# A three-step gate on the output projection of a four-batch attention and MoE block

## The reference, cut to what matters

```python
h = _layernorm(x) * (1 + ca) + sa
x = x + ga * attention(h)            # out @ out_w + out_b at its end
h = _layernorm(x) * (1 + cb) + sb
x = x + gb * ffn(h)                  # top-4 routing, 16 experts, shared expert
```

## Time and profile before

| what | value |
|---|---|
| median of three runs | 3380.76 us |
| the profiled execution | 3378.87 us |
| its span, first to last instruction | 3377.1 us |
| PE busy | 88% of the span |
| DVE, ACT, POOL busy | 66%, 53%, 39% |
| mean granted TensorE clock | 0.939 |
| mean DMA rate | 106 GB/s |

### The profile page before, as it was taken

The page is one execution under the profiler, slowest core; times in us unless marked ns, Lnnn a source line. Parts: engine busy times, 40 slices in busy tenths (PEclk is TensorE's granted clock), DMA queues, the critical chain, the costliest instruction groups (busy, mean ns, idle before and its releaser), DMA issues.

```text
span 3377.1 us, 61010 instructions
## 1 busy us (share of the span) xinstructions
PE 2970.4 (88%) x22500; PEld 1632.5 (48%) x22500; DVE 2242.5 (66%) x5047; ACT 1782.1 (53%) x2736; POOL 1311.7 (39%) x1685
## 2 busy tenths in 40 slices
PE   7787799999999999999988878888877799999886
PEld 4433233334333333333333222227876788999775
DVE  7887498888788877999877756413821124655465
ACT  3322456665666655666544545664644465666322
POOL 6755112134322145211357446334045514441355
PEclk9988899999999999999989878998989899999998
DMA  4833512232222223122324332134355545564465
GB/s 162 209 99 101 116 33 57 62 79 63 68 60 63 60 57 92 43 38 61 76 87 127 93 97 84 51 126 143 91 161 166 163 124 167 179 182 143 143 178 150
DMA packets 290690, 359.05 MB, mean 106 GB/s; under 512 B 65404, under 2 KB 243212, under 8 KB 290140
## 3 DMA queue, kind: packets, MB, share of 16 engines
q1 hardware_dynamic: 259516, 279.94, 30.3%
q0 software_dynamic: 30208, 71.87, 7.0%
q10 hardware_dynamic: 672, 3.34, 0.4%
HBM read 206.25 MB, written 139.21 MB: 102 GB/s over the span
## 4 chain that ended last, share of the span: by engine, by line
PE 52%; DVE 12%; ACT 9%; issue 7%; POOL 3%; DMA 3%; SPq 3%; another core or an unknown queue 2%; POOLq 0%; ACTq 0%; DVEq 0%
PE PB L1139 12%; PE PB L1066 8%; PE PB L1155 8%; ACT P L1615 8%; DVE mx L1434 7%; PE PB L1013 6%; PE PB L1036 5%; PE PB L1049 5%; PE PB L1124 2%; PE PB L1080 2%; DMA ON<-osb 1%; SPq L844 1%; PE PB L1103 1%; POOL P L1762 1%
## 5 line engine op out<-in xcount | busy, mean ns | idle before, releaser
L1434 DVE TENSOR_REDUCE mx<-PB 128x1 f32<-128x512 f32 (+3 forms) x2560 | 1405.8, 603 | 293.1 <-PE PB L1013 155.5
L1615 ACT ACTIVATE P<-PB 128x1024 f32<-128x1024 f32 (+3 forms) x1280 | 1097.8, 894 | 791.9 <-PE PB L1049 771.7
L1013 PE MATMUL PB<-KO,QO 64*128 64x512 bf16 (+3 forms) x2560 | 782.2, 359 | 81.6 <-DVE mx L1434 56.5
L1066 PE MATMUL PB<-P,V 128*17 128x512 f32 (+3 forms) x5120 | 617.7, 555 | 15.6 <-POOL P L1762 15.6
L1036 PE MATMUL PB<-QO,KO 64*128 64x512 bf16 (+3 forms) x2560 | 550.7, 359 | 54.4 <-ACT P L1615 28.9
L1049 PE MATMUL PB<-QO,KO 34*128 34x512 bf16 (+3 forms) x2560 | 543.0, 359 | 42.7 <-remote 29.5
L1013 PEld LDWEIGHTS PB<-KO,QO 64*128 64x128 bf16 x2560 | 205.5, 94 | 769.7 <-DVE mx L1434 545.0
L1545 DVE TENSOR_TENSOR haT<-sl,PB 64x128 f32<-64x128 f32 x350 | 101.4, 290 | 556.7 <-ACT sl L1694 357.7
L1139 PE MATMUL PB<-xT,ws 128*128 128x128 f32 x3432 | 451.3, 284 | 19.3 <-issue 10.7
L1139 PEld LDWEIGHTS PB<-xT,ws 128*128 128x128 f32 x3432 | 425.1, 200 | 23.8 <-issue 13.0
L1762 POOL TENSOR_SCALAR_AFFINE_SELECT P<-P 128x256 f32<-128x256 f32 x512 | 205.3, 410 | 572.6 <-ACT P L1615 568.4
(11 more groups left out here) (179 smaller groups left out, 3328.5 us busy)
## 6 DMA issues: line engine op xcount, KB each, us to landing
xq<-x_slots SPq DMA_DIRECT2D x286, 128.0 KB
qk_parts<-pt SPq DMA_DIRECT2D x192, 128.0 KB, 2.4
KO<-qk_parts SPq DMA_DIRECT2D x192, 128.0 KB, 3.8
y_slots<-yo SPq DMA_DIRECT2D x191, 128.0 KB
QO<-qk_parts SPq DMA_DIRECT2D x64, 256.0 KB, 3.6
rden<-rden_rows SPq DMA_DIRECT2D x256, 64.0 KB
y_slots<-mx SPq DMA_DIRECT2D x95, 128.0 KB
v_rows<-vst SPq DMA_DIRECT2D x16, 544.0 KB, 3.5
```

Source lines behind the costliest of these rows:

```text
L1013: mm = pe.matmul(PB[:, bank, 0:n], QO[half, k3, j, 128 * t:128 * t + 128], KO[half, k3, j, 512 * kc:512 * kc + n], start=True, stop=True)
L1066: mm = pe.matmul(PB[32 * j:32 * j + 17, 7, c0:512], V[:, g % 2, kt, 17 * j:17 * j + 17], P[:, pbuf(g, i, j // 2), j % 2, 0:n], start=kt == ...
L1434: dve.tensor_reduce(mx[:, j, t, kc:kc + 1], PB[:, u.bank[item], 0:n], AX.X, ALU.max).then_inc(s["mx"], 1)
L1615: act.activation(P[:, pbuf(g, i, p), :, 0:n], PB[:, 2 * p:2 * p + 2, 0:n], ACT.Exp, scale=0.25).then_inc(s["exp"], 1)
```

## The change: what it does

A fourth item is put on `late`, called "packed", due 14 ticks after the chunk's last pv, three after "pack". No engine emits anything for it: it is only a mark in the list. `project(b)` now holds back o_proj of a tile until the mark "packed" of the batch's last group (gi = 3) stands in the list, and no longer until "pack" does. While it holds back, it yields, and the pump's unit for that call is spent on nothing.

```diff
@@ plan(), project(b)
-                    while stages[d] == "o_proj" and not o.has("pack", b, 3, (it - d) // 4):
+                    while stages[d] == "o_proj" and not o.has("packed", b, 3, (it - d) // 4):
                         yield
                     unit(stages[d], b, it - d)
                     yield
@@ plan(), values(g, i)
             late.append([10, [("on", g // 4, g % 4, c)]])
             late.append([11, [("pack", g // 4, g % 4, c)]])
+            late.append([14, [("packed", g // 4, g % 4, c)]])
```

## The result

| | before | after |
|---|---|---|
| median of four runs | 3375.29 us | 3323.26 us (3314.03 to 3331.89) |
| the profiled execution, its span | 3377.1 us | 3323.3 us |
| mean granted clock | 0.939 | 0.946 |

A fourth run of the kernel before stands beside the three of the first table, so its median is 3375.29 us here. The ratio of the runs is 0.9836, 95% interval 0.981 to 0.9861: 52 us are gained by the medians, between 47 and 64 by the interval, against a forecast of 61. The median lies 6 us above the forecast of 3317 us and inside the range of 3298 to 3344.

A forecast was written before the change was run, and what follows sets the result against it. PE, busy 88% of the span, was taken to bound the kernel. Idle 38.3 us plus clock 24.1 us gave 62.4 us; 3378.87 less this, plus 1 for group 11's end, gave 3317 us, range 3298 to 3344.

The forecast's parts named there:

- The 12 stalls and their places: At the projection, PE waits for packing DMAs at tiles 0, 4 and 12 in four batches; all 12 should go.
- The spare time at the tightest gate: At the projection's gates, three loops of 7.68 us against the longest wait, 5.9 us, leave at least 1.8 us.
- Idle, 38.3 us: PE's 12 waits for packing at the projection, by the matmul records: 38.3 us to be saved.
- clock, 24.1 us: In the 5 us behind each of 12 stalls, granted clock averages 0.598; restoring full clock saves 24.1 us.
- The cross-check of one stall: Tile 0's stall against the same loops of group 5: 4.1 us, 4.4 by the sum, perhaps 4 us too high in all.
- after the worst: The 5 us window behind the stall taken as the worst was read as having a granted clock of 0.50.
- rival (c): Groups 13 and 14 grow by PE's remote waits as the scatter shifts: 3341 us (8%), or 3396 us (3%).
- The end of group 11: PE waits 3.78 us for a mask behind POOL's zero-fill wait; shift bounded minus 3.8 to plus 6, taken plus 1.
- (a): At the projection, the waits go but the clock stays low: only 38.3 us saved, 3341 us; chance 7%.
- (b): At tile 12, packing moves with the projection as SP waits longer; four stalls partly stay, 3337 us; chance 9%.
- (d): At tile 0, something moving with the projection holds PE, not packing; no change, 3379 us; 7% with small mixtures.
- (e): More is saved, by the 72 us bound or luck in groups 13 and 14: 3300 us; chance 8%.

The follow-up runs named there:

- e3: Kernel after with the mark "packed" due 13 ticks after the last pv in place of 14: 3342.66 us, 0.9838 of the kernel before.
- e1: Kernel after with the mark due 10 ticks after the last pv in batches 0 to 2, 11 in batch 3: 3435.80 us, 1.011 of before.
- e4: The kernel after, unchanged (mark at 14 ticks), repeated on the first set's chip: 3342.08 us, 0.982 of the kernel before.
- e7: Kernel before with useless matmuls on PE ahead of its packing wait at tiles 0, 4 and 12: 3130.48 us, 0.9923 of before.
- e10: The kernel after, unchanged, repeated on the third set's chip: 3094.22 us, 0.9811 of the kernel before.
- e9: Kernel before with three empty units ahead of the first half's routing, shifting routing, zero fill and scatter but not the projection: 1.0006 of before.
- e2: Kernel after with the mark due 12 ticks after the last pv in place of 14: 3359.63 us, 0.9898 of the kernel before.
- e11: Kernel after with seven empty units between the first half's zero fill and the first indirect DMA waiting for it: 3082.88 us, 0.9778 of before.
- e5: Kernel after with only the gate of tiles 0 to 3 waiting for the later mark, others for "pack": 3100.10 us, 0.9829 of before.
- e6: Kernel after with only the gate of tiles 12 to 15 waiting for the later mark, others for "pack": 0.9913 of before.
- e12: Kernel after with the mark due 17 ticks after the last pv in place of 14: 3082.52 us, 0.978 of the kernel before.

## Why the prediction was right

**The 12 stalls and their places.** The count of calls put the projection's gates on loops 16, 25, 39 and 12, and after the change on 19, 28, 3 and 15, and at job 13. The lists of items of both kernels have them there (in batch 3, tile 8 stands at job 0 in place of loop 3). All 12 waits went. The spare time at the tightest gate was put at 1.8 us or more; e3 shows it from the other side: one loop less leaves 0.8 us of idle in one place only.

**Idle, 38.3 us, and clock, 24.1 us.** That both terms are real is shown: the series e1 to e4 changes the idle, the filler of e7 takes the clock term alone. Their sum is confirmed less sharply than 66.7 against 62.4 looks. Stretch by stretch the sum, idle plus clock, has 16.1, 17.0, 14.3 and 14.1 us; measured were 14.1, 17.5, 21.1 and 14.0. The first two repeat: groups 3 and 4 take 235.8, 234.2 and 235.7 us in the three profiles of the kernel after (after, e4, e10), groups 7 and 8 240.8, 241.1 and 241.1. The last two do not. In e4 groups 11 and 12 took 261.5 us in place of 255.5, and from group 15 to the end 1208.3 in place of 1188.1, which is more than the kernel before had. That these two came out at 21.1 and 14.0 is in part luck.

A second pair are e9, whose projection stands where that of the kernel before does, and e10, both on one chip. The same working gives 36.0 us of idle and 22.4 us of clock for e9, 58.4 in all; the four stretches gained 13.9, 15.7, 16.4 and 7.6 us, 53.6 in all, and the medians differ by 60.1. The cross-check of one stall, which found the sum some 4 us too high, points the same way.

One reading of the rows was loose: the window with a clock of 0.50 is called the one "after the worst" stall, but it stands behind 3.40 us of idle, and the two waits of 5.37 us have 0.65 and 0.51. The clock that is lost does not follow the length of the wait; in e2 the 5 us behind a wait of 1.44 us have a clock of 1.00, where those behind 1.20 us in the kernel before have 0.66. The 2 us per stall are a mean of these 12 and no price of every stall.

**What the sum left out.** Against the 66.7 stand 13.2 us lost where no stall was. 5.5 us of it lie ahead of group 3, where nothing was changed; this part takes anything from 688.7 to 696.2 us in the profiles here, and 695.3, 692.1 and 691.2 in the three of the kernel after. The other 7.7 us lie in groups 13 and 14, which was the mild form of rival (c). Group 14 alone took 137.1, 135.9 and 139.6 us in the three profiles with the scatter shifted by two loops (after, e3, e4) and 128.7, 131.4 and 131.6 in the three without (before, e1, e2), all on chips where the kernel takes the longer of its times (the last section tells of them). GpSimd's wait for the rows that it scatters (Rsg<-h_rows) goes the same way, 69.9, 83.4 and 81.8 us against 42.1, 59.0 and 66.4. That points to a cost of about 7 us of the shift there. It is not shown: e3's two groups together took 283.7 us where 289 was expected, e4's took 294.0, e2's 282.9 where 281 was, and e9, which would have told, ran on a chip without these waits.

**The end of group 11.** The step allowed plus 1 us for PE's wait behind the zero fill. It was 4.91 us in the profile after against 3.78. Right, but the working only asked what the shift adds. It did not ask what the whole wait was worth, and that was the next 11 us (e11).

**The rivals.** (a), a clock that stays low, is out: the windows of groups 3 to 8 have 0.99. The rule of the Trainium skill that stood beside it ("TensorE: Matmul & The Clock Gate", section "A second HAM failure mode: psum-queue depth-cycling") does not carry over to this kernel. In groups 5 and 6 of the kernel before the weight loads wait 100 times for DVE, 0.9 us at most, and the clock is 1.00 there:

```profile
PEld PB L1013 <- DVE mx L1434: 62.4, 100, 0.9
```

(b) is out by the timeline of SP at tile 12, and in all batches by the list of waits. (d) is out by e5 and e6: which stalls come back depends on the gate alone. (c) came in its mild direction, 7.7 us and not 24, and (e) did not come.

## What to carry to other kernels

Where an order is written out ahead, give a consumer its place by when its data lands, not by when its transfer is issued; here one wait of 3 us on the bounding engine cost about 5 on average, because the engine also lost its clock behind it. A gate at the head of a pumped pipeline shifts all that follows, so look first whether one gate is enough, and place it no earlier than the first point where the idle is gone. Later points are worth a run too: here three loops more gave another 12 us, most of it for a reason that stays open. Then look for the same pattern on the other in-order engines: here a GpSimd instruction that waited 8.15 us for a transfer held up the masks behind it, and PE with them.

## What the runs showed of the hardware

The same kernel takes 3402 us on one chip and 3152 and 3156 on two others. In the profile after and in that of e10 the code is the same; the windows of groups 13 and 14 and of the stage from the end of attention differ, first in the profile after, then in e10:

```profile
1846.20:1998.10 151.90, 113.42 (x932) 37.40 (x931) 91.10 (x172) 71.08 (x86) 83.68 (x108) 0.84 0.39 105
1998.10:2135.20 137.10, 112.75 (x886) 35.33 (x889) 81.47 (x151) 69.58 (x84) 67.56 (x92) 0.85 0.23 72
2236.20:3323.30 1087.10, 936.94 (x6406) 854.38 (x6406) 493.52 (x1466) 532.42 (x1210) 422.76 (x452) 0.93 0.51 155
```
```profile
1845.40:1953.60 108.20, 100.58 (x937) 36.02 (x938) 89.03 (x171) 70.23 (x85) 83.70 (x108) 0.95 0.54 148
1953.60:2059.10 105.50, 96.72 (x883) 32.74 (x882) 80.67 (x152) 69.30 (x85) 67.19 (x91) 0.97 0.30 93
2162.70:3094.50 931.80, 880.82 (x6405) 816.09 (x6406) 491.64 (x1466) 534.85 (x1210) 423.34 (x452) 0.98 0.60 180
```

Groups 5 and 6 take 101.0 us on all of them; the difference of 230 us lies in the stages with the scatter's and the experts' transfers. The profile after has waits of PE for a releaser that it calls remote:

```profile
PEld PB L1050 <- remote: 46.4, 20, 12.2
PE PB L1050 <- remote: 38.3, 18, 11.7
```

e5 to e12 have no such wait at all. So the loss in groups 13 and 14, on which rival (c) was priced, does not come from the kernel alone. It goes with the chip, or with its state at the time: each chip ran in one set only, and so these two are not told apart. What the queue behind "remote" carries, the profile does not say; it stays open. The gain of the change is nearly the same on all: 0.9836, 0.982 and 0.9811 of before.
